# A two-layer graph network on one core: edge terms of the multi head made by TensorE during pooling and loaded from DRAM, running sums added in PSUM, x kept in SBUF

## The reference, cut to what matters

```python
h = relu(layernorm(x))
logit = tanh(h @ W1.T) @ w2                       # pooling: softmax of logit[src] per dst
x = x + segment_sum(softmax(logit[src]) * h[src], dst)
h = relu(layernorm(x))
# multi head: 8 heads of 16, e = edge_attr @ We0
alpha = sum(q[dst] * (k[src] + e)) / 4
h = relu(segment_sum(softmax(alpha) * (v[src] + e), dst) + h @ Ws0 + bs0)
# single head: the same with one head of 128, no relu behind it
x = x + segment_sum(softmax(alpha1) * (v1[src] + e1), dst) + h @ Ws1 + bs1
```

## Time and profile before

| | us |
|---|---|
| median of 3 runs | 10818.31 |
| lowest, highest | 10810.28, 10887.77 |
| span of the profiled execution, first to last instruction | 7414.1 |

### The profile page before, as it was taken

The page is one execution under the profiler, slowest core; times in us unless marked ns, Lnnn a source line. Parts: engine busy times, 40 slices in busy tenths (PEclk is TensorE's granted clock), DMA queues, the critical chain, the costliest instruction groups (busy, mean ns, idle before and its releaser), DMA issues. The chain is left out here.

```text
span 7414.1 us, 172328 instructions
## 1 busy us (share of the span) xinstructions
PE 5718.3 (77%) x38285; PEld 4085.0 (55%) x38285; DVE 4663.7 (63%) x12926; ACT 3438.6 (46%) x8180; POOL 4576.5 (62%) x4707
## 2 busy tenths in 40 slices
PE   4555566666665688888888888856889999999998
PEld 3455555555542466666666666633555556666666
DVE  4444555555665788999999999933444555555542
ACT  3233333333443466666666666612444444444441
POOL 0777777777750477777666665502777777777630
PEclk7777878888986799999999999977999999999995
DMA  2334444444434666666655555534445555555532
GB/s 81 85 82 83 85 85 87 88 89 89 92 90 140 161 155 157 159 158 153 151 144 145 142 140 137 130 103 119 108 110 112 117 116 119 123 122 123 119 88 60
DMA packets 1267854, 861.45 MB, mean 116 GB/s; under 512 B 637234, under 2 KB 1158320, under 8 KB 1266840
## 3 DMA queue, kind: packets, MB, share of 16 engines
q1 hardware_dynamic: 1091672, 438.53, 25.3%
q0 software_dynamic: 175168, 411.90, 23.7%
HBM read 780.46 MB, written 69.42 MB: 115 GB/s over the span
## 5 line engine op out<-in xcount | busy, mean ns | idle before, releaser
L757 POOL DMA_INDIRECT ring_multi<-kv_rows,src_cols x1564 | 1609.3, 1029 | 1029.7 <-issue 440.4
L1155 POOL DMA_INDIRECT ring_single<-h_rows,src_cols x1564 | 1482.6, 948 | 857.2 <-issue 480.3
L1155 POOL DMA_INDIRECT ring_pool<-pool_rows,src_cols x1564 | 1482.0, 948 | 678.6 <-issue 451.5
L1258 PE MATMUL ps_s_pool<-ident,row_pool 128*128 128x128 f32 x1952 | 365.1, 319 | 718.0 <-ACT row_pool L1300 716.8
L1300 ACT ACTIVATE row_pool<-ring_pool 128x520 f32 x488 | 309.1, 633 | 1162.1 <-POOLq L1146 1162.1
L958 PE MATMUL ps_e_multi<-w_edge,attrT 64*128 64x512 f32 x976 | 544.5, 638 | 331.4 <-DVE kv L847 310.9
L1222 DVE CUSTOM_DVE_ANT_0 masked_pool<-mask_pool,ps_s_pool,start_pool 128x512 f32<-128x512 bf16 x488 | 364.8, 748 | 633.4 <-PE ps_s_pool L1258 552.3
L1271 PE MATMUL ps_p_pool<-row_pool,probT_pool 128*128 128x129 f32 x3904 | 667.1, 325 | 55.2 <-DVE probT_pool L1235 54.2
L847 DVE TENSOR_TENSOR kv<-ring_multi,ps_e_multi 128x1024 f32<-128x1024 f32 x488 | 596.1, 1222 | 161.6 <-issue 124.0
L1258 PEld LDWEIGHTS ps_s_pool<-ident,row_pool 128*128 128x128 f32 x1952 | 254.1, 160 | 801.5 <-issue 764.9
L1305 ACT ACTIVATE rowT<-ps_r 128x512 f32<-128x512 f32 x488 | 291.7, 598 | 816.4 <-PE ps_r L1265 816.4
(11 more groups left out here) (218 smaller groups left out, 12218.1 us busy)
## 6 DMA issues: line engine op xcount, KB each, us to landing
dst_pool<-in_dst_rows SPq DMA_DIRECT2D x488, 128.0 KB
dst_multi<-in_dst_rows SPq DMA_DIRECT2D x488, 128.0 KB
dst_single<-in_dst_rows SPq DMA_DIRECT2D x488, 128.0 KB
query_multi<-query_parts SPq DMA_DIRECT2D x488, 96.0 KB
cols<-query_cols SPq DMA_DIRECT2D x488, 64.0 KB
ring_pool<-pool_rows,src_cols POOLq DMA_INDIRECT x1564
ring_multi<-kv_rows,src_cols POOLq DMA_INDIRECT x1564
ring_single<-h_rows,src_cols POOLq DMA_INDIRECT x1564
```

The costliest lines, as they stand in the source:

```text
L757: pool.indirect_dma_start(out=ring[:, u, j, :], out_offset=None, in_=rows, in_offset=bass.IndirectOffsetOnAxis(ap=g.src_cols[:, c:c + 1], ...
L1155: pool.indirect_dma_start(out=ring[:, u, j, :], out_offset=None, in_=rows, in_offset=bass.IndirectOffsetOnAxis(ap=g.src_cols[:, c:c + 1], ...
L1258: i = T_.transpose(ps_s[p1][:, j * P:(j + 1) * P], row[:, u1, j, D + 1:D + 2].to_broadcast([P, P]), g.ident[:])
```

## The change

x is loaded once, in `prepare`, into a tile that stays (`x_rows`), and every later stage adds to it there: no load of x in the hidden stage and in projection, no x1 and skip2 rows in DRAM, and the output is stored from it. The edge terms of the multi head (512 x 128 per block) are made by PE in the pooling stage, at the end of each of its first 391 items, copied out by ACT and stored in DRAM (`edge_terms`, 102.5 MB); the multi head's SP loads one per item (256 KB) in place of the edge attributes, and the kv add takes it from SBUF. The running sums of the multi head, scaled by DVE, go to a tile `kept_sums`, PE adds them to the block's sums in PSUM by a matmul with the identity, and ACT copies the result to `acc`. `acc` is cleared by POOL in the stages between and no more by DVE at the front of the edge stages. In projection, fold and output PE turns batch n before it multiplies batch n - 1, with two buffers, DVE works a batch ahead, fold multiplies by weights folded beforehand (one product less), and the output's seven 17-column transposes become one of 119.

```diff
+        g.x_rows = sb(g, ctx, "x_rows", [P, NODE_TILES, D])
+        g.x_loaded = [sem(g, f"x_loaded{k}") for k in range(BATCHES // 2)]
...
+            for n in range(BATCHES):
+                sp.dma_start(g.x_rows[:, n * ROWS_B:(n + 1) * ROWS_B], rows_of(t["x"], n)).then_inc(g.x_loaded[n // 2], 16)
...
+            pool.memset(g.acc[:], 0.0)
...
-            for n in range(BATCHES):
-                D_["stats"].wait(sp, n - LOADS)
-                sp.dma_start(acc[:, n * ROWS_B:(n + 1) * ROWS_B, 0:D], rows_of(t["x"], n))\
-                  .then_inc(loaded[n % LOADS], 16)
...
-                    E["attrT" if multi else "partial"].wait(sp, n - U)
-                    sp.dma_start(attr[:, u], t["edge_attr_16"].rearrange("(k p) c -> p k c", p=P)[:, ds(b * J, J), :])\
+                    E["rel"].wait(sp, n - QB)
+                    sp.dma_start(dst[:, u % QB], t["dst_rows"][ds(b, 1), :].to_broadcast([P, EDGES_B]))\
                       .then_inc(g.attrs_loaded[u], 16)
-                    E["rel"].wait(sp, n - U)
-                    sp.dma_start(dst[:, u], t["dst_rows"][ds(b, 1), :].to_broadcast([P, EDGES_B]))\
-                      .then_inc(g.attrs_loaded[u], 16)
+                    E["kv"].wait(sp, n - EB)
+                    sp.dma_start(term[:, u % EB].rearrange("p j c -> p (j c)"),
+                                 g.edge_terms[ds(b, 1)].rearrange("a p c -> (a p) c"))\
+                      .then_inc(terms_loaded[u % EB], 16)
...
-            V.memset(g.run_max[:], -BIG)
+            V.memset(g.run_max[:], -BIG).then_inc(g.acc_clear, 1)
...
-                    V.tensor_tensor(out=a5h, in0=a5h, in1=factor[:, f5].unsqueeze(2).to_broadcast([P, H, HW]),
+                    V.tensor_tensor(out=kept_sums[:, (u - 5) % 2].rearrange("p (h c) -> p h c", h=H), in0=a5h,
+                                    in1=factor[:, f5].unsqueeze(2).to_broadcast([P, H, HW]),
                                     op=ALU.mult).then_inc(E["scaled"].sem, 1)
...
-                    E["edge"].wait(dve, m1)
+                    dve.wait_ge(terms_loaded[m1 % EB], 16 * (m1 // EB + 1))
                     E["message"].wait(dve, m1 - 4)
                     dve.wait_ge(blocks_ready, items.block(m1) + (1 + blocks_base))
                     V.tensor_tensor(out=kv[:, u1 % 4],
                                     in0=in_ring(items.block(m1), 0, 2 * D).rearrange("p j (a c) -> p j a c", a=2),
-                                    in1=ps_e[:].rearrange("p (j c) -> p j c", j=J).unsqueeze(2)
+                                    in1=term[:, m1 % EB].unsqueeze(2)
                                     .to_broadcast([P, J, 2, D]), op=ALU.add).then_inc(E["kv"].sem, 1)
                 items.prepare(n + 1)
...
-                if has(m5, ITEMS):
-                    a5 = a5.rearrange("p t c -> p (t c)")
-                    E["partial"].wait(dve, m5)
-                    if multi:
-                        E["scaled"].wait(dve, m5)
-                        i = V.tensor_tensor(out=a5, in0=a5, in1=ps_p[:, 0:acc_w], op=ALU.add)
-                    else:
-                        E["factor"].wait(dve, m5)
-                        E["summed"].wait(dve, m5 - 1)
-                        i = V.scalar_tensor_tensor(out=a5, in0=a5, scalar=factor[:, f5, 0:1],
-                                                   in1=ps_p[:, 0:acc_w], op0=ALU.mult, op1=ALU.add)
-                    i.then_inc(E["summed"].sem, 1)
...
-                        i = T_.matmul(ps_p[:, 0:acc_w], lhs, rhs, start=(j == 0), stop=(j == J - 1))
-                    i.then_inc(E["partial"].sem, 1)
-                if multi and has(n, ITEMS):
-                    loaded(pe, g.attrs_loaded, attrs_base, n, u, 32)
-                    E["onehot"].wait(pe, n - 1)
-                    T_.transpose(ps_s[0:J * EDGE_DIM, 0:P], attr[:, u].rearrange("p j c -> p (j c)"),
-                                 g.ident[:]).then_inc(E["attrT"].sem, 1)
-                if multi and has(n, ITEMS):
-                    E["attrT_sb"].wait(pe, n)
-                    E["kv"].wait(pe, n - 1)
-                    T_.matmul(ps_e[:], attrT[:, u % 2], w_edge[:].rearrange("k j c -> k (j c)"),
-                              start=True, stop=True).then_inc(E["edge"].sem, 1)
+                        T_.matmul(ps_p[:, 0:acc_w], lhs, rhs, start=(j == 0), stop=False)
+                    E["scaled"].wait(pe, m5)
+                    T_.matmul(ps_p[:, 0:acc_w], g.ident[:], kept_sums[:, p5], start=False, stop=True)\
...
-                    E["attrT"].wait(act, n)
-                    E["edge"].wait(act, n - 2)
-                    S_.activation(attrT[:, u % 2], ps_s[0:J * EDGE_DIM, 0:P], ACT.Copy)\
-                      .then_inc(E["attrT_sb"].sem, 1)
...
+                if has(m5, ITEMS):
+                    E["partial"].wait(act, m5)
+                    S_.activation(g.acc[:, ds(items.tile(m5), 1), 0:acc_w].rearrange("p t c -> p (t c)"),
+                                  ps_p[:, 0:acc_w], ACT.Copy).then_inc(E["summed"].sem, 1)
...
+                k = n - STORE_LAG
+                if not single and 0 <= k < BLOCKS:
+                    sp.wait_ge(term_copied, k + 1)
+                    sp.dma_start(g.edge_terms[k], term[:, k % EB]).then_inc(term_stored[k % EB], 16)
+                if not single and n < BLOCKS:
+                    if n >= EB:
+                        sp.wait_ge(term_made, n - EB + 1)
+                    sp.dma_start(attr[:, n % EB], t["edge_cols"][0:EDGE_DIM, n * EDGES_B:(n + 1) * EDGES_B])\
...
-            V.memset(g.acc[:], 0.0)
...
+                if not single and n < BLOCKS:
+                    if n == 0:
+                        pe.wait_ge(g.w_edge_loaded, 16)
+                    pe.wait_ge(attr_loaded[n % EB], 16 * (n // EB + 1))
+                    if n >= 2:
+                        pe.wait_ge(term_copied, n - 1)
+                    for j in range(J):
+                        i = T_.matmul(ps_e[n % 2][:, j * D:(j + 1) * D], attr[:, n % EB, j * P:(j + 1) * P], w_edge[:],
+                                      start=True, stop=True)
+                    i.then_inc(term_made, 1)
...
+                k = n - 1
+                if not single and 0 <= k < BLOCKS:
+                    act.wait_ge(term_made, k + 1)
+                    if k >= EB:
+                        act.wait_ge(term_stored[k % EB], 16 * (k // EB))
+                    S_.activation(term[:, k % EB], ps_e[k % 2][:], ACT.Copy).then_inc(term_copied, 1)
...
-                sp.dma_start(xb[:, n % XB], rows_of(t["x"], n)).then_inc(loaded[n % XB], 16)
...
-                    D_["x_sum"].wait(sp, n)
-                    sp.dma_start(rows_of(g.x1_rows, n), xb[:, n % XB]).then_inc(stored[n % XB], 16)
...
+            for n in range(BATCHES):
+                D_["x_sum"].wait(pool, n)
+                pool.memset(acc[:, n * ROWS_B:(n + 1) * ROWS_B, :], 0.0)
...
+                    x1 = xr[:, n * ROWS_B + j]
+                    i = V.scalar_tensor_tensor(out=x1, in0=sums[:, j, 0:D], scalar=den[:, u, j:j + 1], in1=x1,
+                                               op0=ALU.mult, op1=ALU.add)
...
+                if has(n + 1, BATCHES):
+                    summed(n + 1)
...
+            for n in range(BATCHES + 1):
+                if has(n, BATCHES):
+                    D_["hidden"].wait(pe, n)
+                    D_["turned_sb"].wait(pe, n - 1)
+                    for j in range(ROWS_B):
+                        i = T_.transpose(ps_h[:, j], h[:, n % 2, j], ident[:])
+                    i.then_inc(D_["turned"].sem, 1)
+                k = n - 1
+                if has(k, BATCHES):
+                    D_["turned_sb"].wait(pe, k)
+                    for j in range(ROWS_B):
+                        i = k * ROWS_B + j
+                        evac.wait(pe, i - 6)
+                        T_.matmul(ps_z[i % 6][:], hT[:, k % 2, j], w[:].rearrange("p a n -> p (a n)"),
+                                  start=True, stop=True).then_inc(D_["product"].sem, 1)
...
+                D_["acc_read"].wait(pool, n)
+                pool.memset(batch(acc, n), 0.0)
...
-                    sp.dma_start(x1[:, u], rows_of(g.x1_rows, n)).then_inc(loaded[u], 16)
...
-                    sp.dma_start(rows_of(g.skip2_rows, k), x1[:, v]).then_inc(stored[v], 16)
...
+                    V.tensor_tensor(out=x1, in0=x1, in1=bs[:].unsqueeze(1).to_broadcast([P, ROWS_B, D]), op=ALU.add)\
                      .then_inc(D_["weighed"].sem, 1)
...
+            T_.matmul(ps_q[:, 0:2].rearrange("p a n -> p (a n)")[:, 0:ACC_W], wqT[:], folded[:], start=True, stop=True)
...
-                for a, b in halves:
-                    i = T_.matmul(flat(ps_q, a, b), wq[:], flat(hT, a, b), start=True, stop=True)
-                i.then_inc(D_["q_turned"].sem, 1)
...
+                        i = T_.matmul(flat(ps_q, a, b)[0:TAIL], both[:, D:ACC_W], flat(hT[:, v], a, b), start=True, stop=True)
+                    i.then_inc(D_["q_turned"].sem, 1)
```

(15 more changed lines are left out.)

547 lines of the change are left out of this document (273 added, 274 removed).

## The result

The kernel after takes 10233.16 us (median of 4 runs, 10225.50 to 10238.19), the kernel before beside it 10814.30 (10789.00 to 10887.77): a ratio of 0.9441, 95% interval 0.9407 to 0.9476, a gain of 581 us. The forecast was 10600, with 10480 to 10730 as its range. The direction was right and the size was not.

A forecast was written before the change was run, and what follows sets the result against it. Pooling was taken as bound by POOL, multi head by POOL then DVE, single head finally by PE, dense stages mostly by transfers. +17 + 0 - 80 + 30 - 125 - 60 = -218 from 10818 gave 10600 us, range 10480 to 10730.

The forecast's parts named there:

- The sum against the span, carried to the median: Whole kernel: stage changes summed against the 7414.1 us span; the 3404 us up to the 10818.31 us median taken over unchanged.
- Its own sign of being wrong: Whole kernel: a difference between time and span other than 3404 us would show the forecast wrong.
- lies outside the span: Outside the traced span: the new 102 MB scratch tensor could add or take time in either direction; 6%.
- Multi head, +30: Multi head: gathers held by the kv add at 5.95 us per block, then DVE at 4.55 per item; +30, bounds -83 and +80.
- the first rival: Multi head: the kv add does not hold the gathers, so it gains 83 us instead of losing 30; 10487 us in all; 20%.
- Projection, -80: Projection: no load or store of x, 13.8 us per batch, 220 us in all; -80, bounds -50 and -110.
- Fold, -125: Fold: x1 load, skip2 store and one product go; 8.5 us per batch plus 27, 146 in all; -125, bounds -90 and -150.
- Output, -60: Output: seven tail transposes become one, pipeline doubled, 154 us; -60, bounds -40 and -120 (half the matmul time at full clock).
- the alternation of 128 and 17 rows: Output: alternating 128 and 17 rows might space the matmuls; without it, less than 11.8 us per batch.
- Pooling, 0: Pooling: making, copying and storing the edge terms fits beside POOL's pace of 5.0 us per block; 0, bounds 0 and +40.
- Preparation and hidden, +17: Preparation and hidden: x loads delay the row_scratch stores, +20, with some 3 back in hidden; +17, bounds 0 and +25.
- Single head, 0: Single head: untouched but for a 12 us memset at its front, covered by a ring of 8 blocks; said to end PE-bound.

The follow-up runs named there:

- r17: Kernel after with the kv add's second input from a PSUM tile of zeros (edge terms missing), on a 7.4 ms chip: multi head 2310 us against 2362.
- r18: Kernel after, but multi head makes its own edge terms, pooling none, sums still by PE; on a 7.4 ms chip: 7000 us, 0.946 of before's 7397.
- r7: Kernel after, unchanged, on a 7.4 ms chip: 7098 us, against 7405 for the kernel before beside it.
- r8: Kernel after with the multi head's own edge terms, none in pooling, and sums added by DVE, on a 7.4 ms chip: 7063 us.
- r11: Kernel after with the multi head's own edge terms, none in pooling, sums by DVE, on a slow chip: 10427 us against 10816 for before, 0.9660.
- r13: Kernel after with the kv add's second input from a PSUM tile of zeros (edge terms missing), on a slow chip: multi head 3464 us against 3316.
- r10: Kernel before, unchanged, traced on a slow chip: 10851 us.
- r9: Kernel after without the second product of the single head's score, on a 7.4 ms chip: single head 2074 us against 2078.

## Why the prediction was right or wrong

- *The sum against the span, carried to the median.* This is the step that failed: "Everything in them is taken over unchanged, and the sum is made against the span." The 3404 us were not outside the span. They are waits inside the edge stages on chips B, and the change took some 370 us of them away in one of those stages. Against the 637 us of the table the forecast of 218 misses 419: 397 in the multi head, 39 in fold and 48 in the output, while pooling and the single head take 72 back. Its own sign of being wrong, a difference between time and span other than 3404, came: it is 2 us. The doubt I gave it, 6% for what "lies outside the span", named the wrong place: a scratch tensor, not the stages.
- *Multi head, +30.* On A +6, at the paces that were forecast: 5.80 us per block for the predicted 5.95 in its first half, 111 items in the 500 us from 3800, or 4.50 us, for the predicted 4.55. But both sides of the balance are about half as large as they were taken: 46 to 52 us gained while the kv add reads PSUM (r17, r18) where the first rival had 83, and 52 to 54 lost with the second SBUF input where 113 were taken (from -83 to +30). That the net came near is partly luck. PE's share, taken to fall to 65%, was 77% (1820.10 of 2362 us), at a granted clock of 0.84 for 0.95. On B -367, where signals of TensorE come late, which no trace of the forecast showed.
- *Projection, -80.* -82 on A, -81 on B. The sum is right and its steps nearly: the product takes 1.07 us per tile (105.2 us for 98, r7) where 1.27 was taken, the normalising 2.8 us per batch (39.0 us for 14) where it was 2.3.
- *Fold, -125.* -163, outside its bounds of -90 to -150; 8.1 us per batch as a whole, where I had 8.5 and 27 us of start and end that are not there.
- *Output, -60.* -107 on A, -108 on B. Two terms were sized too small, the clock (0.88 granted against 0.53 in the earlier trace rows) and the step of a matmul. A matmul that stepped by 0.72 us steps by 0.22:

```profile
7035.82 0.39 PE L1785 MATMUL ps_z<-wv,sT 128*128 128x128 f32 x2
7036.04 0.39 PE L1786 MATMUL ps_z<-wt,tT 119*128 119x128 f32 x2
```

  The traces tell the two apart. In the kernel before the step is 0.42 in the few stretches of full clock, and in the kernel after 0.43 in those of half clock:

```profile
7253.44 0.48 PE L1747 MATMUL ps_z<-wt,tT 17*128 17x128 f32 x2
7253.86 0.49 PE L1746 MATMUL ps_z<-wv,sT 128*128 128x128 f32 x2
```

```profile
7007.21 0.64 PE L1786 MATMUL ps_z<-wt,tT 119*128 119x128 f32 x2
7007.64 0.63 PE L1785 MATMUL ps_z<-wv,sT 128*128 128x128 f32 x2
```

  So the new order of matmuls took the step from 0.72 to 0.43 at half clock, 58 us over 14 batches of 14, and the clock from 0.43 to 0.22, at most 40 more. The bound of -120 was the clock alone; the forecast named the alternation of 128 and 17 rows as what might space the matmuls and gave it little. Whether the 119 rows alone did it was not tried.
- *Pooling, 0.* +38 on A, at the edge of its bounds; without the edge terms (r8) the stage is 1981. On B the terms cost 61 us on B2 (2929 in r11, 2990 in r13) and 76 on B1, beyond them. On A (r7) POOL's waits for landings are the new entry, 52.7 us:

```profile
L1133 POOL DMA_INDIRECT ring_pool<-pool_rows,src_cols x1564 | 1479.5, 946 | 661.6 <-issue 459.7 <-POOLq L409 134.6 <-DMA ring_pool<-pool_rows,src_cols 52.7
```

- *Preparation and hidden, +17.* +11 on both. *Single head, 0.* +6 on A; +21 on B between two chips, +2 on B2 (3209 in r10, 3211 in r13). That it "ends bound by PE" was read wrongly: with 416 us less of PE's busy time (r9) it took 2074 for 2078.
- *Outside the span.* 2 us in every run. The 102 MB cost nothing there.

Had the time been that of chip A, the forecast of -218 would stand against a measured -293 by the spans (7389 to 7096) or -307 by the times (7405 to 7098): inside the stated range, at the edge of the bounds of -300 to -120, with fold and output under-sized by 85 us together.

## What to carry to other kernels

When a kernel's span and its time differ, find out why before summing anything: a trace from one chip cannot be carried to a time from another by adding the difference. Where an engine's completions come late, look at the rounds of signals per item before the busy time: on B removing 606 us of PE's busy time gave back 138, and the change, with two rounds fewer and one moved, gained 10% of a stage in which PE was busy for 70% (though not shown to be by the rounds alone). And an instruction that gets a second SBUF input should be charged to POOL's gathers too, not only to its own engine.

## What the runs showed of the hardware

- The same kernel took 7.4 ms on two chips and 10.6 to 10.8 ms on three. Stages of transfers and dense products agree within 1%; the three edge stages differ by 49% to 57%.
- On one of the three (r10) 31% of TensorE's recorded signals in the multi head and 43% in the single head come over 1 us after the recorded (modelled) end of the matmul; DVE's and ACT's do not.
- With a DVE add of 1024 columns that has two SBUF inputs in place of one, gathers beside it are longer: 1110 ns for 1047 and 1162 for 1112 on average, and the stage 52 us of 2362.
- The output stage with fewer and shorter gaps of PE had the clock granted at 0.88 instead of 0.53. Its matmuls stepped by 0.43 us at half clock and 0.22 at full, those of the kernel before by 0.72 and 0.42.
